# Layer 0 of a four-layer graph network: the one-hots of four edge tiles from one comparison, tiles innermost

## The chip, the cores and the metric

The kernel runs on one core of one Trainium2 chip. The metric is the device time of one execution in microseconds (us). Engines are called as in the profile: PE is TensorE's matrix unit, PEld its weight loads, DVE is VectorE, ACT is ScalarE, POOL is GpSimd, SP is SyncE.

## The reference

Four graph layers run one after the other over 6,250 nodes with 128 features and 206,250 edges sorted by destination; after each, the result is added to the features and normalised. The change lies in the first layer (layer 0), which averages the features of each node's sources:

```python
agg = segment_sum(x[src], dst, num_segments=n)
deg = segment_sum(ones(src.shape[0]), dst, num_segments=n)
mean_neigh = agg / maximum(deg, 1.0)[:, None]
out = x @ w_self.T + b_self + mean_neigh @ w_neigh.T + b_neigh
x = layernorm(x + out)
```

Layer 1 runs an MLP over each edge and sums it by destination, layer 2 sums node and edge features over neighbours, layer 3 is graph attention with four heads. They are the same before and after.

## The kernel before

The edges are cut into NT = 1612 tiles of 128 edges (one edge per partition), the nodes into NB = 49 blocks of 128. Since edges are sorted by destination, a tile touches only S = 7 destination slots. GT = 18 tiles make a group with 18 x 7 = 126 slots; there are NS = 90 groups.

Layer 0 doesn't gather. For each tile `q` it builds two one-hot matrices in bf16 and multiplies them. `hotU` (128 edges x 128) marks the source's row within its block (`src & 127`, called `low`). `hotV` (128 edges x 343) marks the pair of source block and slot (`(src >> 7) * 7 + slot`, less `CMID`, called `code`). Their product on TensorE, `dense_adjacency` (L662), is a 128 x 343 matrix of edge counts in PSUM. ScalarE copies it into the group's matrix `AT` in `dense_counts` (L642). When the 18 tiles of a group are there, `dense_sums` (L681) multiplies that matrix with the node features: 49 matmuls of 258 columns for a group, spread over the next 18 tiles, so that each tile has two or three of them behind its L662. GpSimd stores each group's matrix to DRAM (`atab`, L773) for layer 2; `AT` has two buffers, so ScalarE's first copy of group s waits for the store of group s-2.

Each engine runs one loop over the place `q`, in an order written out by hand. At place q VectorE makes the hots of tile q (L622 and L624), and at fixed distances the steps of the nodes' tail (division, residual, norm: L695 to L719), the group's small sums (L655) and its node one-hots (L558). The hots sit in a ring of NU = 8 tiles: VectorE waits for the adjacency matmul of tile q-8 (`d.adj`) before it writes tile q, TensorE for both hots of q (`d.hot`) and for the copy out of one of three PSUM banks (`d.count`). `codes` (L600 to L609) makes `low` and `code` as float32 for 18 tiles in five instructions, at the middle of the group before. At the even places 10 to 26 VectorE also makes the low halves of the features (L790, nine parts). Before all this, the prologue splits the features (L385, L391), casts the two ranges `ioc` and `iob` to bf16 (L375, L376) and prepares bias rows (L395, L397, L401).

The two instructions that make the one-hots of a tile compare a bf16 range with one scalar for each partition:

```python
e.tensor_scalar(hotU[:, q % NU, :], iob[:, :], low[:, s % 2, i:i + 1], None, ALU.is_equal)
e.tensor_scalar(hotV[:, q % NU, 0:S * NB], ioc[:, :], code[:, s % 2, i:i + 1], None, ALU.is_equal)
```

Of the kernel before, what the change touches and what calls it, by code (L numbers as in the profile page):

```python
# [9 lines left out]
I32 = mybir.dt.int32  # L10
FR = mybir.dt.float32r
BF = mybir.dt.bfloat16
ALU = mybir.AluOpType
ACT = mybir.ActivationFunctionType
AX = mybir.AxisListType
P = 128
G = 4
# [3 lines left out]
S = 7  # L21
GT = P // S
# [7 lines left out]
def plan(n_nodes, n_edges, n_rand):  # L30
    nb = -(-n_nodes // P)
    nt = -(-n_edges // (P * G)) * G
    lo, hi = [], []
    for b in range(nb):
        ends = []
        for d, sign in ((b * P, -1), (min((b + 1) * P, n_nodes), 1)):
            q = d / n_nodes
            mean = d + n_rand * q
            ends.append(mean + sign * (5 * (n_rand * q * (1 - q)) ** 0.5 + 2))
        lo.append(max(0, int(ends[0] // P)))  # L40
        hi.append(min(nt, int(-(-ends[1] // P))))
    lo[0], hi[-1] = 0, nt
    first = [min(b for b in range(nb) if lo[b] <= t < hi[b]) for t in range(nt)]
    last = [max(b for b in range(nb) if lo[b] <= t < hi[b]) for t in range(nt)]
    return nb, nt, lo, hi, first, last


def groups(nt, first, last):

    ns = -(-nt // GT)  # L50
    return ns, [first[GT * s] for s in range(ns)], [last[min(GT * s + GT, nt) - 1] for s in range(ns)]
# [53 lines left out]
def build(nc, n_nodes, n_edges, n_rand, a, out):  # L105
    NB, NT, LO, HI, FIRST, LAST = plan(n_nodes, n_edges, n_rand)
    NS, B0, B1 = groups(NT, FIRST, LAST)
# [5 lines left out]
    NEA = 5  # L113
    ND = 5
    NK = 4
    NU = 8
    CMID = S * NB // 2
    CB = 6
    NCB = -(-NB // CB)
# [7 lines left out]
    END = [min(GT * s + GT, NT) - 1 for s in range(NS)]  # L127
# [6 lines left out]
    with ctx:  # L134
        def sb(name, shape, dt=F32, c=ctx):
            return c.enter_context(nc.sbuf_tensor(name, shape, dt))

        def sem(name):
            return ctx.enter_context(nc.semaphore(name))
# [14 lines left out]
        slot = sb("slot", [P, NS * GT])  # L154
# [2 lines left out]
        hs = sb("hs", [P, NB, HB])  # L157
        nd = sb("nd", [P, NB, 4])
        am = sb("am", [P, 8])
        iob = sb("iob", [P, P], BF)  # L160
        ioc = sb("ioc", [P, S * NB], BF)
        iota = sb("iota", [P, 256])
        npcol = sb("npcol", [P, NB])
        oh2 = sb("oh2", [P, ND, 256], FR)
# [67 lines left out]
        s_mid = sem("s_mid")  # L232
# [19 lines left out]
        mid = sb("mid", [P, S * NB], c=pre)  # L252
        odd = sb("odd", [P, GT], c=pre)
        hflat = hs[:, :, :].rearrange("p a b -> p (a b)")
# [3 lines left out]
        def x_part(c):  # L258
            return slice(CB * c, min(CB * c + CB, NB))
# [73 lines left out]
        def prep_vector(e):  # L333
# [38 lines left out]
            e.tensor_scalar(node[0:SL, :], node[0:SL, :], small[0:SL, 0:1], None, ALU.add).then_inc(s_prep_v, 1)  # L372
            e.tensor_scalar(par[:, 1:2], par[:, 0:1], -1.0, 1.0, ALU.mult, ALU.add).then_inc(s_prep_v, 1)
            e.wait_ge(s_mid, 1)
            e.tensor_copy(ioc[:, :], mid[:, :]).then_inc(s_mid, 1)  # L375
            e.tensor_copy(iob[:, :], iota[:, 0:P]).then_inc(s_mid, 1)  # L376

            e.wait_ge(s_x, 16)
            for c in range(NCB + 1):
                if c < NCB:  # L380
                    b = x_part(c)
                    u = over0[:, c % 2, 0:(b.stop - b.start) * P].rearrange("p (b f) -> p b f", f=P)
                    if c >= 2:
                        e.wait_ge(s_xhi, 2 * c - 1)
                    e.scalar_tensor_tensor(out=u, in0=xs[:, b, :], scalar=SPLIT, in1=xs[:, b, :], op0=ALU.mult,  # L385
                                           op1=ALU.subtract).then_inc(s_xhi, 1)
                if c:
                    b = x_part(c - 1)
                    u = over0[:, (c - 1) % 2, 0:(b.stop - b.start) * P].rearrange("p (b f) -> p b f", f=P)
                    e.wait_ge(s_xhi, max(1, 2 * c - 2))  # L390
                    e.scalar_tensor_tensor(out=xhl[:, b, 0:128], in0=xs[:, b, :], scalar=SPLIT, in1=u, op0=ALU.mult,  # L391
                                           op1=ALU.subtract).then_inc(s_xhi, 1)
# [57 lines left out]
        with nc.Block() as block:  # L450
            block.gpsimd(prep_pool)
            block.sync(prep_sync)
            block.vector(prep_vector)
            block.tensor(prep_tensor)
            block.scalar(prep_scalar)
# [3 lines left out]
        def expected():  # L459
# [22 lines left out]
            held1 = sb("held1", [P, NK, 2, 384], FR, c=l1)  # L482
            over1 = sb("over1", [P, 2, 384], c=l1)
            l1.close()
            o = NU * (P + 352) // 2
            gint, low, code = (hflat[:, o + 2 * GT * i:o + 2 * GT * (i + 1)].rearrange("p (u c) -> p u c", u=2)
                               for i in range(3))
            gint = gint.bitcast(I32)
            l3 = ExitStack()
            hots = sb("hots", [P, GT, S], c=l3)  # L490
            pk = sb("pk", [P, GT, 4], c=l3)
# [26 lines left out]

            rv1 = view(NR1, 384)
            hbf = hflat.bitcast(BF)  # L520
            hotU = hbf[:, 0:NU * P].rearrange("p (n c) -> p n c", n=NU)
            hotV = hbf[:, NU * P:NU * (P + 352)].rearrange("p (n c) -> p n c", n=NU)
            ADJ = bank[1], bank[4], bank[5]
            AT = tuple(at0[:, i, :].rearrange("p (b c) -> p b c", c=SL) for i in range(2))
            rv3 = ring[:, :].rearrange("p (t f) -> p t f", f=HROW)
# [65 lines left out]

            def codes(e, d, s):

                n = END[s] - GT * s + 1
                c = slice(GT * s, GT * s + n)
                if s:
                    e.wait_ge(d.code, 5 * s)
                e.tensor_scalar(gint[:, 0, 0:n], src[:, c], P - 1, None, ALU.bitwise_and).then_inc(d.code, 1)  # L600
                e.tensor_scalar(gint[:, 1, 0:n], src[:, c], 7, None, ALU.arith_shift_right).then_inc(d.code, 1)
                if s >= 2:
                    e.wait_ge(d.hot, 2 * (END[s - 2] + 1))
                e.wait_ge(d.code, 5 * s + 2)
                e.tensor_copy(low[:, s % 2, 0:n], gint[:, 0, 0:n]).then_inc(d.code, 1)
                e.scalar_tensor_tensor(out=code[:, s % 2, 0:n], in0=gint[:, 1, 0:n], scalar=float(S), in1=slot[:, c],
                                       op0=ALU.mult, op1=ALU.add).then_inc(d.code, 1)
                e.wait_ge(d.code, 5 * s + 4)
                e.tensor_scalar(code[:, s % 2, 0:n], code[:, s % 2, 0:n], -float(CMID), None, ALU.add).then_inc(d.code, 1)  # L609

            def dense_hots(e, d, q):
                if q == 0:
                    codes(e, d, 0)
                elif q % GT == GT // 2 and q // GT + 1 < NS:
                    codes(e, d, q // GT + 1)
                if q < NT:
                    s, i = q // GT, q % GT
                    if i == 0:
                        e.wait_ge(d.code, 5 * s + 5)
                    if q >= NU:  # L620
                        e.wait_ge(d.adj, q - NU + 1)
                    e.tensor_scalar(hotU[:, q % NU, :], iob[:, :], low[:, s % 2, i:i + 1], None, ALU.is_equal).then_inc(  # L622
                        d.hot, 1)
                    e.tensor_scalar(hotV[:, q % NU, 0:S * NB], ioc[:, :], code[:, s % 2, i:i + 1], None,  # L624
                                    ALU.is_equal).then_inc(d.hot, 1)

            def dense_blank(e, d, q):
                n = END[NS - 1] - GT * (NS - 1) + 1
# [27 lines left out]

            def dense_adjacency(e, d, q):
                if q < NT:
                    e.wait_ge(d.hot, 2 * q + 2)
                    if q >= 3:  # L660
                        e.wait_ge(d.count, q - 2)
                    e.matmul(ADJ[q % 3][:, 0:S * NB], hotU[:, q % NU, :], hotV[:, q % NU, 0:S * NB], start=True,  # L662
                             stop=True).then_inc(d.adj, 1)

            LAG0 = 1
# [115 lines left out]
            def vector0(e):  # L781
                e.wait_ge(s_src, 16)
                e.wait_ge(s_mid, 3)
                e.wait_ge(s_prep_v, 31)
                e.memset(xhl[:, :, 256:YW].bitcast(F32), 1.0).then_inc(s_ones0, 1)
                for q in range(N0):
                    c = (q - LOW0) // 2
                    if (q - LOW0) % 2 == 0 and 0 <= c < NCB:
                        b = x_part(c)
                        e.tensor_tensor(xhl[:, b, 128:256], xs[:, b, :], xhl[:, b, 0:128].bitcast(F32), ALU.subtract).then_inc(  # L790
                            s_xlo, 1)
                    dense_hots(e, d0, q)
                    dense_blank(e, d0, q)
                    if q - 8 in KEEPS0:
                        halves_added(e, d0, KEEPS0[q - 8])
                    if q in NODES0:
                        node_hots(e, NODES0[q], d0.node, d0.add, ND, B1[max(0, NODES0[q] - ND)] + 1)
                    for b, k in W0.get(q, []):
                        vector_post0(e, b, k)
# [9 lines left out]
            def tensor0(e):  # L809
                e.wait_ge(s_ones0, 1)  # L810
                for q in range(N0):
                    dense_adjacency(e, d0, q)
                    dense_sums(e, d0, q)
                    for b in LASTS.get(ADDS0.get(q), []):
                        add_nodes(e, b, 129, 128, d0.node, d0.kept, 1, s_mean0, 6, d0.add)
                    for b, k in W0.get(q, []):
                        tensor_post0(e, b, k)
# [979 lines left out]
        with nc.If(strays == 0):  # L1797
            expected()
# [67 lines left out]
```

## Time and profile before

| | us |
|---|---|
| median of three runs | 6451.55 |
| lowest and highest | 6450.44, 6462.29 |
| span of the profiled execution, from its first to its last instruction | 5707.4 |
| median less the span (before the first and after the last instruction) | 744.15 |
| layer 0's adjacency matmuls, from the first to the last start | 50.0 to 948.1 |

The profiled execution has no time of its own on record beside its span, so the working is made against the span and carried over to the median: whatever the span gains or loses, the median does. Layer 0 takes some 900 us of the span; layer 1 follows to about 3,040, layer 2 to about 3,640, and layer 3 fills the rest. In a timeline the starts of two neighbouring instructions tell the engine's pace; the time of one is longer than the pace, since instructions overlap in the pipeline.

### The profile page before, as it was taken

What the parts mean: (1) busy time and instruction counts of PE and PEld (TensorE: products, weight loads), DVE (VectorE), ACT (ScalarE), POOL (GpSimd) and SP (SyncE); (2) the same over time, 40 slices, a digit from 0 to 9 for tenths busy, and PEclk for the clock granted to TensorE, in tenths of its full rate; (3) what the DMA queues carried; (4) which work ended last, traced back from release to release, by engine and by line L of the source; (5) the groups of instructions that cost most, each with busy time, mean ns of one, the idle gap of its engine ahead of it and who ended that gap; (6) DMA issues with size and microseconds to landing.
All of it is one profiled execution on the core that took longest, in us unless ns stands there. A gap on an engine that the chain in (4) does not pass through costs nothing.

```text
span 5707.4 us, 76723 instructions
## 1 busy us (share of the span) xinstructions
PE 4531.6 (79%) x25589; PEld 3717.3 (65%) x25589; DVE 2795.5 (49%) x10327; ACT 1993.7 (35%) x4098; POOL 3118.8 (55%) x3336
## 2 busy tenths in 40 slices
PE   6999998999999999999998999644545544544544
PEld 5999997667677777767768999634444444444444
DVE  8999996333333333433345444333443443443444
ACT  5888886222222222222224555211111121111112
POOL 0000002777777777777770000377777777777775
PEclk9999999999999999999999999777777777677777
DMA  6777777777767777777766777422222222222221
GB/s 153 170 167 165 165 168 178 210 212 210 210 210 211 209 212 208 212 208 212 209 189 191 243 244 246 123 55 56 56 56 56 56 56 56 56 56 56 57 56 43
DMA packets 479979, 843.08 MB, mean 148 GB/s; under 512 B 73951, under 2 KB 302474, under 8 KB 468074
## 3 DMA queue, kind: packets, MB, share of 16 engines
q0 software_dynamic: 141920, 462.69, 32.3%
q1 hardware_dynamic: 323562, 365.74, 21.0%
q10 hardware_dynamic: 14112, 9.74, 0.5%
q8 instruction: 214, 3.51, 0.2%
q14 instruction: 171, 1.40, 0.1%
HBM read 682.70 MB, written 155.18 MB: 147 GB/s over the span
## 4 chain that ended last, share of the span: by engine, by line
PE 49%; POOL 26%; issue 10%; DMA 7%; DVE 6%; ACT 1%; ACTq 0%; POOLq 0%; DVEq 0%
POOL ring L536 26%; PE bank L1196 9%; PE bank L1028 9%; PE bank L681 8%; PE bank L1015 7%; PE bank L662 4%; DMA ring<-ptab,src 4%; DMA ring<-htab,src 2%; PE bank L1478 2%; PE bank L1514 2%; PE bank L1507 1%; PE bank L576 1%; DVE ring L1405 1%; DMA atab<-at 1%; PE bank L1485 1%
## 5 line engine op out<-in xcount | busy, mean ns | idle before, releaser
L536 POOL DMA_INDIRECT ring<-htab,src x1612 | 1527.4, 947 | 503.1 <-issue 472.2
L536 POOL DMA_INDIRECT ring<-ptab,src x1612 | 1526.8, 947 | 498.6 <-issue 440.7
L1028 PE MATMUL bank<-ring,oh 128*126 128x384 f32 x3224 | 1213.7, 488 | 0.0
L982 DVE TENSOR_TENSOR ring<-bank,ring 128x512 f32<-128x512 f32 x806 | 529.9, 685 | 1231.8 <-DMA ring<-ptab,src 1227.7
L1015 PE MATMUL bank<-w1e,ea 128*128 128x256 f32 x3224 | 845.7, 385 | 46.2 <-DVE ring L982 37.3
L998 ACT ACTIVATE ring<-ring 128x1024 f32<-128x1024 f32 x403 | 425.6, 1056 | 1252.8 <-DVE ring L982 1252.8
L1015 PEld LDWEIGHTS bank<-w1e,ea 128*128 128x128 f32 x3224 | 601.1, 190 | 354.0 <-DVE ring L982 119.8
L681 PE MATMUL bank<-xhl,at 128*126 128x258 f32 x4410 | 815.3, 325 | 1.0 <-ACT at L642 1.0
L1514 PE MATMUL bank<-ring,oh 128*126 128x132 f32 x3224 | 589.8, 316 | 244.9 <-DVE ring L1405 244.3
L642 ACT ACTIVATE at<-bank 128x343 fp32r<-128x343 f32 x1612 | 731.2, 489 | 140.7 <-PE bank L662 61.6
L1028 PEld LDWEIGHTS bank<-ring,oh 128*126 128x126 f32 x3224 | 589.8, 188 | 199.8
L1514 PEld LDWEIGHTS bank<-ring,oh 128*126 128x126 f32 x3224 | 492.2, 215 | 333.1 <-DVE ring L1405 314.7
L681 PEld LDWEIGHTS bank<-xhl,at 128*126 128x126 f32 x4410 | 695.6, 192 | 3.5 <-ACT at L642 1.2
L1470 PE MATMUL bank<-ident,pk 128*72 128x128 f32 x90 | 38.4, 427 | 753.5 <-ACT pk L1428 753.5
L1196 PE MATMUL bank<-yhl,adj 128*126 128x256 f32 x4410 | 565.3, 286 | 11.8 <-DVE yhl L1085 11.8
L1196 PEld LDWEIGHTS bank<-yhl,adj 128*126 128x126 f32 x4410 | 538.4, 188 | 14.7 <-DVE yhl L1085 10.5
L773 POOL DMA_DIRECT2D atab<-at x90 | 51.0, 567 | 892.3 <-ACT at L642 892.3
L662 PE MATMUL bank<-hs 128*128 128x343 bf16 x1612 | 515.8, 321 | 16.0 <-DVE hs L624 8.6
L1470 PEld LDWEIGHTS bank<-ident,pk 128*72 128x72 f32 x90 | 12.2, 136 | 776.6 <-ACT pk L1428 776.6
L624 DVE TENSOR_SCALAR hs<-ioc,hs 128x343 bf16<-128x343 bf16 x1612 | 492.3, 305 | 0.0
L622 DVE TENSOR_SCALAR hs<-iob,hs 128x128 bf16<-128x128 bf16 x1612 | 401.1, 249 | 43.9 <-PE bank L662 30.3
L1054 POOL MEMSET oh<- 128x4788 f32 x1 | 4.1, 4088 | 643.9 <-PE bank L1196 643.9
(268 smaller groups left out, 5298.0 us busy)
## 6 DMA issues: line engine op xcount, KB each, us to landing
atab<-at POOLq DMA_DIRECT2D x90, 1543.5 KB, 9.6
ring<-ea_r SPq DMA_DIRECT2D x403, 256.0 KB, 4.0
ea<-ea_t SPq DMA_DIRECT2D x403, 256.0 KB, 3.1
adjb<-atab SPq DMA_DIRECT2D x180, 535.5 KB, 4.7
adjb<-atab SPq DMA_DIRECT2D x90, 472.5 KB, 4.2
ring<-ptab,src POOLq DMA_INDIRECT x1612, 3.5
ring<-htab,src POOLq DMA_INDIRECT x1612, 2.5
ptab<-pO ACTq DMA_DIRECT2D x49, 128.0 KB, 4.6
```

Of the source, the lines that this page charges most:

```text
L536: return e.indirect_dma_start(o, None, table, bass.IndirectOffsetOnAxis(ap=src[:, t:t + 1], axis=0))
L622: e.tensor_scalar(hotU[:, q % NU, :], iob[:, :], low[:, s % 2, i:i + 1], None, ALU.is_equal).then_inc(d.hot, 1)
L624: e.tensor_scalar(hotV[:, q % NU, 0:S * NB], ioc[:, :], code[:, s % 2, i:i + 1], None, ALU.is_equal).then_inc(d.hot, 1)
L642: e.activation(AT[s % 2][:, :, S * i:S * i + S], ADJ[t % 3][:, 0:S * NB].rearrange("p (b j) -> p b j", j=S), ACT.Copy).then_inc(d.count, 1)
L662: e.matmul(ADJ[q % 3][:, 0:S * NB], hotU[:, q % NU, :], hotV[:, q % NU, 0:S * NB], start=True, stop=True).then_inc(d.adj, 1)
L681: m = e.matmul(SUM[g % 2][0:SL, 0:YW], AT[g % 2][:, h, :], xhl[:, h, :], start=h == 0, stop=h == NB - 1)
L982: e.tensor_tensor(group1(gi, m % 2), MLP[m % 3][:, :].rearrange("p (g f) -> p g f", g=2), group1(gi, m % 2), ALU.add).then_inc(s_edge, 1)
L998: e.activation(group1(gi), group1(gi), ACT.Relu).then_inc(s_relu, 1)
L1015: w = e.matmul(MLP[m % 3][:, 256 * i:256 * i + 256], ea[:, gi % NEA, 2 * h + i, :], w1e[:, :], start=True, stop=True)
L1028: e.matmul(SUM[s % 2][0:SL, 0:384], slots_of(s, i), rv1[:, t // G % NR1, t % G, :], start=i == 0, stop=t == END[s]).then_inc(s_sum1, 1)
L1196: m = e.matmul(SUM[g % 2][0:SL, 0:256], adj[:, u % 3, c * SL:c * SL + SL], yhl[:, h, :], start=h == 0, stop=h == NB - 1)
L1514: e.matmul(SUM[g % 2][0:SL, 0:HROW], slots_of(g, k), rv3[:, t % (NRING * G), :], start=k == 0, stop=t == END[g]).then_inc(s_sum3, 1)
```

## The change

`iob` and `ioc` become 128 x (128 x 4) and 128 x (343 x 4), each value four times in a row. For every fourth tile, two `tensor_tensor` instructions, both operands bf16, compare them with the codes of four tiles at once, so the hots of four tiles lie interleaved, tiles innermost. The ring holds NQ = 3 of these fours, twelve tiles. `low` and `code` are bf16 rows for all 1612 tiles, made in five pieces (64 tiles, then four of 387) at the places 0, 8, 16, 24 and 32. TensorE reads both operands of L662 at a stride of four elements (8 bytes).

```diff
-    NU = 8
+    NQ = 3
+    SEGS = [0, 64] + [64 + -(-(NT - 64) * k // 4) for k in range(1, 5)]
-        iob = sb("iob", [P, P], BF)
-        ioc = sb("ioc", [P, S * NB], BF)
+        iob = sb("iob", [P, P, G], BF)
+        ioc = sb("ioc", [P, S * NB, G], BF)
-            e.tensor_copy(ioc[:, :], mid[:, :]).then_inc(s_mid, 1)
-            e.tensor_copy(iob[:, :], iota[:, 0:P]).then_inc(s_mid, 1)
+            e.tensor_copy(ioc[:, :, :], mid[:, :].unsqueeze(2).broadcast_to([P, S * NB, G])).then_inc(s_mid, 1)
+            e.tensor_copy(iob[:, :, :], iota[:, 0:P].unsqueeze(2).broadcast_to([P, P, G])).then_inc(s_mid, 1)
...
+            def codes(e, d, k):
+                c, n = slice(SEGS[k], SEGS[k + 1]), SEGS[k + 1] - SEGS[k]
+                if k:
+                    e.wait_ge(d.code, 5 * k)
                 e.tensor_scalar(gint[:, 0, 0:n], src[:, c], P - 1, None, ALU.bitwise_and).then_inc(d.code, 1)
                 e.tensor_scalar(gint[:, 1, 0:n], src[:, c], 7, None, ALU.arith_shift_right).then_inc(d.code, 1)
+                e.wait_ge(d.code, 5 * k + 2)
+                e.tensor_copy(low[:, c], gint[:, 0, 0:n]).then_inc(d.code, 1)
+                e.scalar_tensor_tensor(out=codef[:, 0:n], in0=gint[:, 1, 0:n], scalar=float(S), in1=slot[:, c], op0=ALU.mult,
+                                       op1=ALU.add).then_inc(d.code, 1)
+                e.wait_ge(d.code, 5 * k + 4)
+                e.tensor_scalar(code[:, c], codef[:, 0:n], -float(CMID), None, ALU.add).then_inc(d.code, 1)
 
             def dense_hots(e, d, q):
                 if q == 0:
                     codes(e, d, 0)
-                elif q % GT == GT // 2 and q // GT + 1 < NS:
-                    codes(e, d, q // GT + 1)
-                    if q >= NU:
-                        e.wait_ge(d.adj, q - NU + 1)
-                    e.tensor_scalar(hotU[:, q % NU, :], iob[:, :], low[:, s % 2, i:i + 1], None, ALU.is_equal).then_inc(
-                        d.hot, 1)
-                    e.tensor_scalar(hotV[:, q % NU, 0:S * NB], ioc[:, :], code[:, s % 2, i:i + 1], None,
-                                    ALU.is_equal).then_inc(d.hot, 1)
+                if q % 8 == 0 and 1 <= q // 8 < len(SEGS) - 1:
+                    codes(e, d, q // 8)
+                if q < NT and q % G == 0:
+                    k = q // G
+                    e.wait_ge(d.code, 5 * next(i for i in range(1, len(SEGS)) if q < SEGS[i]))
+                    if k >= NQ:
+                        e.wait_ge(d.adj, G * (k - NQ + 1))
+                    for o, i, c, n in ((hotU, iob, low, P), (hotV, ioc, code, S * NB)):
+                        e.tensor_tensor(o[:, k % NQ, :, :], i[:, :, :], c[:, q:q + G].unsqueeze(1).broadcast_to([P, n, G]),
+                                        ALU.is_equal).then_inc(d.hot, 1)
...
-                    e.wait_ge(d.hot, 2 * q + 2)
+                    e.wait_ge(d.hot, 2 * (q // G) + 2)
                     if q >= 3:
                         e.wait_ge(d.count, q - 2)
-                    e.matmul(ADJ[q % 3][:, 0:S * NB], hotU[:, q % NU, :], hotV[:, q % NU, 0:S * NB], start=True,
+                    e.matmul(ADJ[q % 3][:, 0:S * NB], hotU[:, q // G % NQ, :, q % G], hotV[:, q // G % NQ, :, q % G], start=True,
                              stop=True).then_inc(d.adj, 1)
```

## Rows read from the trace of the kernel before

**Rows 1.** The page: its first line, and one of the costliest groups.

```profile
span 5707.4 us, 76723 instructions
...
L982 DVE TENSOR_TENSOR ring<-bank,ring 128x512 f32<-128x512 f32 x806 | 529.9, 685 | 1231.8 <-DMA ring<-ptab,src 1227.7
```

**Rows 2.** Busy time by stretch of layer 0: PE, PEld, DVE, ACT, POOL, clock, DMA.

```profile
48.00:56.00 8.00, 4.62 (x12) 1.24 (x12) 7.20 (x37) 4.17 (x11) 0.00 (x0) 0.50 0.00 1
56.00:64.00 8.00, 4.51 (x14) 1.90 (x14) 8.00 (x26) 4.17 (x11) 0.74 (x1) 0.50 0.12 25
64.00:68.00 4.00, 4.00 (x20) 3.56 (x19) 3.90 (x17) 2.34 (x5) 0.00 (x0) 0.53 1.17 247
68.00:76.00 8.00, 8.00 (x63) 7.20 (x62) 7.83 (x45) 7.11 (x18) 0.71 (x1) 1.00 0.36 76
76.00:950.00 874.00, 866.01 (x6693) 786.73 (x6692) 807.50 (x4254) 743.47 (x1843) 49.55 (x88) 1.00 0.78 167
```

**Rows 3.** Groups of instructions by line, 76 to 950 us.

```profile
L681 PE MATMUL bank<-xhl,at 128*126 128x258 f32 x4289 | 794.0, 325 | 1.0 <-ACT at L642 1.0
L642 ACT ACTIVATE at<-bank 128x343 fp32r<-128x343 f32 x1572 | 713.8, 489 | 129.6 <-PE bank L662 51.2 <-DMA atab<-at 33.6 <-PE bank L681 18.3
L681 PEld LDWEIGHTS bank<-xhl,at 128*126 128x126 f32 x4288 | 676.4, 191 | 3.3 <-ACT at L642 1.2
L662 PE MATMUL bank<-hs 128*128 128x343 bf16 x1570 | 499.8, 318 | 7.0 <-DVE hs L622 3.9 <-ACT at L642 2.6 <-DVE hs L624 0.2
L624 DVE TENSOR_SCALAR hs<-ioc,hs 128x343 bf16<-128x343 bf16 x1567 | 478.6, 305 | 0.0
L622 DVE TENSOR_SCALAR hs<-iob,hs 128x128 bf16<-128x128 bf16 x1567 | 389.9, 249 | 43.8 <-PE bank L662 30.3
L662 PEld LDWEIGHTS bank<-hs 128*128 128x128 bf16 x1570 | 150.9, 96 | 82.7 <-DVE hs L622 5.4 <-DVE hs L624 3.0 <-issue 1.7
```

**Rows 4.** Timeline of PE in the steady part: start, us, instruction.

```profile
503.34 0.32 PE L662 MATMUL bank<-hs 128*128 128x343 bf16 x1
503.38 0.64 PE L681 MATMUL bank<-xhl,at 128*126 128x258 f32 x3
503.86 0.32 PE L662 MATMUL bank<-hs 128*128 128x343 bf16 x1
503.90 0.52 PE L681 MATMUL bank<-xhl,at 128*126 128x258 f32 x2
504.26 0.32 PE L662 MATMUL bank<-hs 128*128 128x343 bf16 x1
```

**Rows 5.** Timeline of PE, one of its longest waits.

```profile
623.83 0.31 PE L662 MATMUL bank<-hs 128*128 128x343 bf16 x1 [1.08 <-ACT at L642]
```

**Rows 6.** Timeline of ACT at the same place.

```profile
623.20 0.48 ACT L642 ACTIVATE at<-bank 128x343 fp32r<-128x343 f32 x1 [1.84 <-DMA atab<-at]
```

**Rows 7.** DMA issues: KB each, median us from issue to landing.

```profile
atab<-at POOLq DMA_DIRECT2D x90, 1543.5 KB, 9.6
```

**Rows 8.** Timeline of DVE in the first places of layer 0.

```profile
48.69 0.11 DVE L600 TENSOR_SCALAR hs<-src 128x18 int32<-128x18 int32 x1
...
49.41 0.25 DVE L622 TENSOR_SCALAR hs<-iob,hs 128x128 bf16<-128x128 bf16 x1
...
52.85 0.17 DVE L600 TENSOR_SCALAR hs<-src 128x18 int32<-128x18 int32 x1
...
53.50 0.25 DVE L622 TENSOR_SCALAR hs<-iob,hs 128x128 bf16<-128x128 bf16 x1
...
53.88 0.95 DVE L790 TENSOR_TENSOR xhl<-xs,xhl 128x768 fp32r<-128x768 f32 x1
54.75 0.25 DVE L622 TENSOR_SCALAR hs<-iob,hs 128x128 bf16<-128x128 bf16 x1
```

**Rows 9.** Timeline of PE: the adjacency matmul of tile 36.

```profile
73.26 0.32 PE L662 MATMUL bank<-hs 128*128 128x343 bf16 x1
```

**Rows 10.** Groups of DVE by line, 0 to 60 us: the wait behind the casts.

```profile
L397 DVE TENSOR_TENSOR hs<-hs,bup 128x896 f32<-128x896 f32 x1 | 1.1, 1093 | 3.3 <-ACT bup L435 3.3
```

More of the change, by code:

```diff
@@ L484, in expected @@
             l1.close()
[L485 to L488, printed above, removed]
+            WHOT = NQ * G * (P + S * NB) // 2
+            LSEG = max(b - a for a, b in zip(SEGS, SEGS[1:]))
+            gint = hflat[:, WHOT + NT:WHOT + NT + 2 * LSEG].rearrange("p (u c) -> p u c", u=2).bitcast(I32)
+            codef = hflat[:, WHOT + NT + 2 * LSEG:WHOT + NT + 3 * LSEG]
             l3 = ExitStack()
@@ L520, in expected @@
             hbf = hflat.bitcast(BF)
-            hotU = hbf[:, 0:NU * P].rearrange("p (n c) -> p n c", n=NU)
-            hotV = hbf[:, NU * P:NU * (P + 352)].rearrange("p (n c) -> p n c", n=NU)
+            hotU = hbf[:, 0:NQ * G * P].rearrange("p (n c g) -> p n c g", n=NQ, g=G)
+            hotV = hbf[:, NQ * G * P:NQ * G * (P + S * NB)].rearrange("p (n c g) -> p n c g", n=NQ, g=G)
+            low, code = (hbf[:, 2 * WHOT + i * NT:2 * WHOT + (i + 1) * NT] for i in range(2))
             ADJ = bank[1], bank[4], bank[5]
@@ L590, in places @@
                 return max(at) + 1, hots, nodes, keeps, adds, at
[L594 to L599, printed above, removed]
+            def codes(e, d, k):
+                c, n = slice(SEGS[k], SEGS[k + 1]), SEGS[k + 1] - SEGS[k]
+                if k:
+                    e.wait_ge(d.code, 5 * k)
                 e.tensor_scalar(gint[:, 0, 0:n], src[:, c], P - 1, None, ALU.bitwise_and).then_inc(d.code, 1)
                 e.tensor_scalar(gint[:, 1, 0:n], src[:, c], 7, None, ALU.arith_shift_right).then_inc(d.code, 1)
[L602 to L609, printed above, removed]
+                e.wait_ge(d.code, 5 * k + 2)
[4 more added lines that the diff above has]
+                e.tensor_scalar(code[:, c], codef[:, 0:n], -float(CMID), None, ALU.add).then_inc(d.code, 1)
             def dense_hots(e, d, q):
@@ L613, in dense_hots @@
                     codes(e, d, 0)
-                elif q % GT == GT // 2 and q // GT + 1 < NS:
-                    codes(e, d, q // GT + 1)
[L616 to L619, printed above, removed]
-                    if q >= NU:
-                        e.wait_ge(d.adj, q - NU + 1)
-                    e.tensor_scalar(hotU[:, q % NU, :], iob[:, :], low[:, s % 2, i:i + 1], None, ALU.is_equal).then_inc(
-                        d.hot, 1)
-                    e.tensor_scalar(hotV[:, q % NU, 0:S * NB], ioc[:, :], code[:, s % 2, i:i + 1], None,
-                                    ALU.is_equal).then_inc(d.hot, 1)
+                if q % 8 == 0 and 1 <= q // 8 < len(SEGS) - 1:
[8 more added lines that the diff above has]
+                                        ALU.is_equal).then_inc(d.hot, 1)
             def dense_blank(e, d, q):
```

## The prediction

> **What bounds the kernel now.** I read the page first: the span is 5707.4 us, the median of the runs 6451.55, so 744.15 us lie outside the span and are touched by nothing here [rows 1]. All edits lie in layer 0, between 48 and 950 us. The table by stretch comes next [rows 2]. The reader is to see two regimes. From 76 to 950 us PE is busy 866.01 of 874.00 us: its idle time there is 8.0 us in all, while DVE is busy 807.50, ACT 743.47. From 48 to 64 us it is the other way round: DVE is busy 15.2 of 16 us, PE 9.1, at a granted clock of 0.50 (1.2 GHz); the clock is back at 1.00 (2.4 GHz) only in the stretch from 68.
>
> Then, whether PE's busy time is its own pace: the PE timeline shows an L662 and three L681 starting over after 0.52 us (503.34 to 503.86), and an L662 with two L681 after 0.40 [rows 4]. So an L681 costs 0.12 us and an L662 0.40 - 0.24 = 0.16. At 2.4 GHz, 258 columns are 0.1075 us and 343 columns 0.143. That is a matmul pace with 0.02 us to spare, not one set by waits. A group of 18 tiles holds 49 L681, 13 threes and 5 twos: (13 x 0.52 + 5 x 0.40) / 18 = 0.487 us a tile.
>
> Last, what the 8.0 us wait for. The groups by line name DVE for part of it [rows 3], but at the longest wait PE stood 1.08 us for ScalarE's copy [rows 5], and that copy had stood 1.84 us for the store of `atab` [rows 6]; ScalarE waits 33.6 us for that store in all [rows 3]. The store lands 9.6 us after its issue [rows 7], and a group lasts 874 / 1570 x 18 = 10.0 us. So the next thing behind PE is the store and the copies, not the one-hots. DVE itself waits 30.3 us for PE: its ring of eight tiles is full [rows 3].
>
> **The change part by part.**
>
> *The hots, from 76 us on.* Before, a tile's pair costs DVE 0.38 us (53.50 to 53.88) [rows 8]. The trace has no 16-bit `tensor_tensor`. Its float32 ones give a slope: 512 elements take 685 ns [rows 1], 768 take 0.95 us [rows 8], so (0.95 - 0.685) / 256 = 1.04 ns an element, and the next instruction starts 0.87 us after a 768 (53.88 to 54.75) [rows 8]: 768 x 1.04 = 0.80, so 0.07 fixed. Upper bound, one element a tick: 512 x 1.04 + 0.07 = 0.60 and 1372 x 1.04 + 0.07 = 1.50, together 2.10 for four tiles, 0.525 a tile. Lower, two a tick: 0.34 + 0.785 = 1.12, 0.28 a tile. The 16-bit L622 and L624 differ by 56 ns for 215 elements [rows 3], 0.26 ns each, four a tick; the engine does pack 16-bit data, so I take two a tick, since a second operand also has to be read. The Trainium skill ("VectorE: DVE Perf Modes", "The perf-mode tier table") gives the bf16 `tensor_tensor` the double rate and no more; no row shows it. DVE then saves 0.10 us a tile, 157 us over 1570 tiles, and the codes' 88 small pieces of 0.65 us (52.85 to 53.50) [rows 8], 57 us. That is worth **nothing**, because PE hides all of DVE's work there. PE's waits there give at most the 8.0 us of idle time back, and I take 0 of them, since their cause is the store.
>
> *Four tiles at a time, ring of twelve.* DVE begins four k when PE has done four k-3, so PE has eight tiles, 8 x 0.487 = 3.9 us, before it needs four k, against 1.12 us of hots. Behind DVE's new wait stand the tail's steps, and their due times are 1 to 10 places from PE's; DVE is now 8 to 12 places ahead, before it was at most 8. Cost 0. If the cover went (hots at 0.525 us), see rival C.
>
> *The start.* Here DVE sets the pace, and the four long code pieces are now all due in it. A small piece costs 0.65 us; 369 more elements cost, at 1.04 ns in all five instructions, 1.92 us more (upper), or at 0.26 ns in the four with one source and 1.04 in the fifth, 0.77 (lower). I take 1.8 us a piece, between 1.42 and 2.57. The first piece, 64 elements, takes the 0.72 us of before (48.69 to 49.41) [rows 8] and 0.14. Sum until the hots of tiles 32 to 35 are there: start 48.69, first piece 0.86, four pieces 7.2, nine fours of hots 9 x 1.12 = 10.1, eight L790 of 0.87 and a short one 7.2: 74.05. PE then does four tiles in 4 x 0.487 = 1.95, and tile 36 starts at 76.0, against 73.26 [rows 9]: **+2.7 us**, between +1.2 and +5.8 by the pieces' bounds. From there PE is the pace again. The hots of tiles 16 to 27 come in bursts, so PE may get its 2.4 GHz later than at 68 us; for each L681 it misses that costs about 0.1 us, and I add **1 us**, between 0 and 4 (some forty of them).
>
> *The casts.* They grow from 471 to 1884 elements in the prologue: at most 1413 x 1.04 = 1.5 us more. Behind them DVE waits 3.3 us for ScalarE's `bup` [rows 10], which covers it: 0. Without that cover it would be 1.5.
>
> *TensorE's strided reads.* No row of this trace has a strided operand on PE. Moving operand: nothing (lower), or each of the 343 columns costs two, 0.143 us a tile, 1612 x 0.143 = 230 us (upper). The nearest row is L681, 4-byte elements side by side at one column a tick: two of our 2-byte elements at 8 bytes' distance span the same 16 bytes as four of those. I take 0, being nearer to a pace that the rows show for half the density. The Trainium skill ("SBUF — State Buffer", "Door 1: The DMA port swizzle") says that SBUF is read in lines of 16 bytes and that two hits in a line suffice for the full rate; eight bytes give just two, and the sum by it is the same 0. Weight load: L662's takes 96 ns, L681's 191 [rows 3]. If the stride makes the first like the second, 0.095 x 1612 = 153 us in full view (upper); but the 191 ns loads lie behind matmuls that follow each other at 0.12 us [rows 4], and L662's load has a 258-column matmul ahead of it, so 0.
>
> Sum: 5707.4 + 2.7 + 1 = 5711.1 for the span, **6455 us** for the median. The own range of this case: 6451.5 + 1.2 - 8.0 = 6445 to 6451.5 + 5.8 + 4 = 6461.
>
> **The rivals.**
>
> *A, TensorE pays a little* (0.08). A load a tenth in view, or a column in ten delayed: 10 to 28 ns a tile, 16 to 45 us, 6472 to 6500. For it: PE has only 0.02 us to spare at L662. It decides from 6 ns a tile on (9 us, with the start over 0.2%).
>
> *B, each column pays* (0.08). The moving read halves: 6455 + 230 = 6685, or half of that, 6570. For it: no row shows a strided read. Against it: the density argument above. The Trainium skill ("Vector Engine (DVE) Microarchitecture Reference", "Measured stream behaviour on trn2") has a rule for VectorE's ports by which only pairs of neighbouring 4-byte words keep the full rate; carried over to TensorE it would be this rival.
>
> *C, the comparison isn't packed* (0.06). The innermost run is only four elements and the codes are a repeated row. Then DVE needs 807.5 + 1570 x 0.145 - 57 = 978 us where PE needs 866: DVE sets the pace, +104 us, and nine fours at 0.98 more, +9 at the start: 6568. It decides where a tile's hots cost more than 0.38 + (874 - 807.5 + 57) / 1570 = 0.46 us.
>
> *D, the other side: faster* (0.07). PE's 0.52 and 0.40 us stand above their columns (0.465 and 0.358) by 0.054 and 0.042 us, up to 80 us in all [rows 4]. If part of that is TensorE held up in SBUF by DVE, which now issues a half instruction a tile for two, it comes back: a third would be 26 us, 6430. Against it: no row shows one engine's reads slowing another's, and the excess may as well be the switch from one matmul to the next. It decides from 0.011 us a tile.
>
> **How the numbers follow.** Main case 0.71, A 0.08, B 0.08, C 0.06, D 0.07. A measurement of this kernel tells 0.2%, 13 us, from no change. The main case gives no change 0.63, slower 0.06, faster 0.02; A, B, C slower 0.22; D faster 0.05 and no change 0.02. Faster 0.07, same 0.65, slower 0.28. The range 6444 to 6500 holds the main case, A and a part of D, about 0.81; B and C lie outside.
>
> **What would show it.** In the changed profile: the hots' `tensor_tensor` near 0.34 and 0.8 us in pace (C: 0.6 and 1.5); DVE's busy time from 76 us down by some 200 us, PE's unchanged near 99%; L662 and three L681 still at 0.52 us (A, B: more; D: less); tile 36 near 76 us; ScalarE's waits for the store of `atab` still there. I am wrong if the pace of 0.52 moves, or if the start costs more than 10 us.

## The result: 6697 us, 3.8% slower

The changed kernel took 6696.68 us (median of four, 6688.77 to 6704.66) against 6451.64 before: a ratio of 1.038, 95% interval 1.0365 to 1.0395. The prediction was no change, 6455 us; the time lies where rival B put it, at 6685 us.

One word on spans first. The chips differ in how fast layers 1 and 3 get their gathered rows: on some the median of the kernel before lies at 6452 to 6469 us, on two others at 5721 and 5723. Its profile [rows 1] has the gathers of the fast kind, where its span is its time but for 5 us; a second profile of it shows that below. So the 744 us that I put outside the span do not exist as such. Layer 0 lasts the same on both kinds: two kernels below whose layers 0 are alike from tile 36 on (`stride2` and `late_codes`) take 882.1 us for it on one kind and 881.9 on the other. Every ratio below is taken on one chip.

The page of the changed kernel begins:

```profile
span 6692.9 us, 74103 instructions
```

Busy time after, first the start and then the rest of layer 0 (PE, PEld, DVE, ACT, POOL, clock, DMA share, GB/s), the answer to [rows 2]:

```profile
68.00:76.00 8.00, 7.12 (x34) 5.93 (x34) 6.96 (x17) 4.19 (x9) 0.00 (x0) 0.65 0.48 101
...
76.00:1190.00 1114.00, 1113.47 (x6711) 910.69 (x6710) 608.05 (x1474) 795.95 (x1849) 46.82 (x88) 1.00 0.61 131
```

The steady part grew from 874 to 1114 us for the same matmuls, at the same granted clock of 1.00. PE is idle for 0.5 us of it, where it was for 8.0. DVE fell from 807.50 to 608.05 us, as forecast. The change did what it does to DVE, and PE, the bound, became slower at the same work. Which part of the work, the groups by line show, beside [rows 3]:

```profile
L679 PE MATMUL bank<-xhl,at 128*126 128x258 f32 x4298 | 1042.0, 377 | 0.5 <-ACT at L640 0.5
...
L640 ACT ACTIVATE at<-bank 128x343 fp32r<-128x343 f32 x1579 | 757.8, 487 | 318.0 <-PE bank L660 246.3 <-PE bank L679 52.2 <-issue 0.3
L660 PE MATMUL bank<-hs 128*128 128x343 bf16 x1579 | 749.0, 474 | 0.0
L622 DVE TENSOR_TENSOR hs<-ioc,hs 128x1372 bf16<-128x1372 bf16 x393 | 340.8, 867 | 0.0
L660 PEld LDWEIGHTS bank<-hs 128*128 128x128 bf16 x1579 | 180.2, 114 | 72.2
L622 DVE TENSOR_TENSOR hs<-iob,hs 128x512 bf16<-128x512 bf16 x393 | 166.8, 424 | 407.8 <-PE bank L660 407.2
```

The adjacency matmul (L660 now, L662 before) went from 318 to 474 ns, its weight load from 96 to 114. ScalarE no longer waits for the store of `atab`: a group now lasts 1114 / 1579 x 18 = 12.7 us, and the store lands 9.4 us after its issue. PE's timeline, against [rows 4]:

```profile
599.97 0.47 PE L660 MATMUL bank<-hs 128*128 128x343 bf16 x1
600.02 0.78 PE L679 MATMUL bank<-xhl,at 128*126 128x258 f32 x3
600.64 0.47 PE L660 MATMUL bank<-hs 128*128 128x343 bf16 x1
600.70 0.66 PE L679 MATMUL bank<-xhl,at 128*126 128x258 f32 x2
601.20 0.48 PE L660 MATMUL bank<-hs 128*128 128x343 bf16 x1
```

L660 and three sums start over after 0.67 us instead of 0.52, with two sums after 0.56 instead of 0.40. L679 is recorded longer (377 ns instead of 325), but its own pace is unchanged: a tile with three sums still takes 0.12 us more than one with two. Below, "pace" is the median of these gaps for tiles with three sums, over the whole layer: 0.519 us before, 0.676 after. The difference, 0.157 us, times 1576 tiles is 247 us; the stalls that went give some 10 back: from tile 36 to the last tile's matmul it takes 1111.75 us against 874.8, 237 more. The start adds 5.0 (tile 36 at 78.25 us, against [rows 9]). Together 242, of the 245 measured.

### The profile page after: what moved, and what is told of

It reads as the page before. It is cut to its first block, busy times and chain, and to the rows that moved or that the text cites. A ratio compares the mean times of both kernels' runs of the same rounds, so it can differ in the third digit from the quotient of the medians.

```text
span 6692.9 us, 74103 instructions
## 1 busy us (share of the span) xinstructions
PE 5056.7 (76%) x25589; PEld 4043.5 (60%) x25589; DVE 2615.9 (39%) x7484; ACT 2045.8 (31%) x4098; POOL 3111.3 (46%) x3336
## 4 chain that ended last, share of the span: by engine, by line
PE 55%; another core or an unknown queue 23%; issue 10%; DVE 9%; ACT 2%; POOL 0%; DMA 0%; ACTq 0%; DVEq 0%
PE bank L1026 12%; PE bank L1013 10%; PE bank L679 8%; PE bank L1194 8%; PE bank L660 7%; PE bank L1512 2%; DVE ring L1403 2%; DVE ring L980 2%; PE bank L578 1%; PE bank L963 1%; PE bank L1476 1%; DVE tops L1258 1%; DVE top L1262 1%; PE bank L1505 0%
## 5 line engine op out<-in xcount | busy, mean ns | idle before, releaser
L679 PE MATMUL bank<-xhl,at 128*126 128x258 f32 x4410 | 1063.3, 376 | 0.5 <-ACT at L640 0.5
L679 PEld LDWEIGHTS bank<-xhl,at 128*126 128x126 f32 x4410 | 818.1, 205 | 130.6 <-ACT at L640 1.1
L1512 PE MATMUL bank<-ring,oh 128*126 128x132 f32 x3224 | 702.3, 364 | 248.1 <-DVE ring L1403 133.8
L1512 PEld LDWEIGHTS bank<-ring,oh 128*126 128x126 f32 x3224 | 602.7, 259 | 340.7 <-DVE ring L1403 176.7
L1026 PEld LDWEIGHTS bank<-ring,oh 128*126 128x126 f32 x3224 | 614.8, 196 | 266.0 <-issue 75.4
L660 PE MATMUL bank<-hs 128*128 128x343 bf16 x1612 | 763.2, 475 | 12.1 <-DVE hs L622 11.9
L1491 PE MATMUL bank<-hs,o2T 128*126 128x4 f32 x346 | 78.0, 329 | 507.3 <-ACT o2T L1441 360.8
L1476 PE MATMUL bank<-rT,sel 72*126 72x128 f32 x720 | 172.8, 416 | 339.6 <-issue 241.9
L1491 PEld LDWEIGHTS bank<-hs,o2T 128*126 128x126 f32 x346 | 73.0, 295 | 525.7 <-ACT o2T L1441 374.0
L1476 PEld LDWEIGHTS bank<-rT,sel 72*126 72x126 f32 x720 | 148.3, 307 | 359.5 <-issue 255.6
L1258 DVE TENSOR_TENSOR tops<-bank,away 126x512 f32<-126x512 f32 x90 | 62.3, 692 | 773.4 <-remote 726.3
```

The costliest lines, as they stand in the source:

```text
L660: e.matmul(ADJ[q % 3][:, 0:S * NB], hotU[:, q // G % NQ, :, q % G], hotV[:, q // G % NQ, :, q % G], start=True, stop=True).then_inc(d.adj, 1)
L679: m = e.matmul(SUM[g % 2][0:SL, 0:YW], AT[g % 2][:, h, :], xhl[:, h, :], start=h == 0, stop=h == NB - 1)
L1026: e.matmul(SUM[s % 2][0:SL, 0:384], slots_of(s, i), rv1[:, t // G % NR1, t % G, :], start=i == 0, stop=t == END[s]).then_inc(s_sum1, 1)
L1476: m = e.matmul(bank[5][0:SL, h * P:(h + 1) * P], sel[0:4 * n, h, :], rT[0:4 * n, :], start=True, stop=True)
L1491: m = e.matmul(bank[7][0:SL, 0:4], o2T[:, b - B0[f], :], hs[:, b, 132:136], start=b == B0[f], stop=b == B1[f])
L1512: e.matmul(SUM[g % 2][0:SL, 0:HROW], slots_of(g, k), rv3[:, t % (NRING * G), :], start=k == 0, stop=t == END[g]).then_inc(s_sum3, 1)
```

## Experiments

**Which operand, or VectorE after all.** Three kernels keep every instruction of the change and alter only where TensorE reads in the four's region. Flat means that an operand's elements are read side by side, and so are a mix of four tiles' one-hots; such a kernel leaves the right counts out.

```diff
+            flatU = hbf[:, 0:NQ * G * P].rearrange("p (n g c) -> p n g c", n=NQ, g=G)
+            flatV = hbf[:, NQ * G * P:NQ * G * (P + S * NB)].rearrange("p (n g c) -> p n g c", n=NQ, g=G)
...
-e.matmul(ADJ[q % 3][:, 0:S * NB], hotU[:, q // G % NQ, :, q % G], hotV[:, q // G % NQ, :, q % G], ...)
+e.matmul(ADJ[q % 3][:, 0:S * NB], flatU[:, q // G % NQ, q % G, :], hotV[:, q // G % NQ, :, q % G], ...)   # weights_flat
+e.matmul(ADJ[q % 3][:, 0:S * NB], hotU[:, q // G % NQ, :, q % G], flatV[:, q // G % NQ, q % G, :], ...)   # moving_flat
+e.matmul(ADJ[q % 3][:, 0:S * NB], flatU[:, q // G % NQ, q % G, :], flatV[:, q // G % NQ, q % G, :], ...)  # both_flat
```

> As the changed kernel, but TensorE reads the stationary operand of L662 (now L662 of this file) as 128 elements side by side from the same four's region, and the moving one still at a stride of four. The one-hots of wrong elements meet, so the counts are not the reference's; every instruction is the same in number and size. Theory M (the moving read pays for each column): a tile with three sums stays near the 0.675 us of the changed kernel, 6685 to 6697 us. Theory W (the strided weight load is what holds TensorE): back to 0.52 us a tile, 6455 us. Both in halves: about 6575 us.

Measured: 6691.86 us against 6469.27, ratio 1.0342 (1.0323 to 1.036), pace 0.665. With no strided weight load nearly the whole cost is still there: theory M. In its timeline a tile with three sums starts over after 0.66 us:

```profile
600.11 0.46 PE L662 MATMUL bank<-hs 128*128 128x343 bf16 x1
...
600.77 0.46 PE L662 MATMUL bank<-hs 128*128 128x343 bf16 x1
```

> The mirror of the run before: the moving operand is read side by side, the stationary one at a stride of four; the counts are not the reference's. Theory M: 0.52 us a tile with three sums, L662 back at 0.32 us, 6450 to 6465 us. Theory W: near 0.675 us and 6697 us. If the weight load's 114 ns instead of 96 come into view, 18 ns a tile, 29 us more: 6485 us.

Measured: 6489.7 us, ratio 1.003 (1.0019 to 1.004), pace 0.538. The matmul is back at 0.34 us and less, and the load's 18 ns come into view in full: 0.019 x 1612 = 31 us, of which the time shows 20, since PE's waits for ScalarE shrink from 6.0 to 1.5 us and ScalarE's for the store from 28.9 to 20.9. This is rival A, in the size it had (10 to 28 ns a tile), but beside the moving operand it is small; with both strided only 0.011 us of it shows (0.676 less 0.665); why not all of it stays open.

> Both operands read side by side; the counts are not the reference's. What is left of the change is VectorE's: hots by fours, the ring of twelve, five code pieces at the start, longer casts. Prediction's own sum: 6455 us, tile 36 near 76 us, between 6445 and 6461. Rival (waiting by fours costs TensorE something, apart from how it reads): above 6465 us.

Measured: 6468.82 us, ratio 0.9999 (0.9989 to 1.0009), pace 0.519. That it lies above the rival's 6465 us is the chip's doing: before takes 6469.27 there. From tile 36 to the last tile it needs 873.5 us, before 874.8, so waiting by fours costs TensorE nothing. Its groups from 76 to 950 us:

```profile
L642 ACT ACTIVATE at<-bank 128x343 fp32r<-128x343 f32 x1577 | 715.5, 489 | 129.2 <-PE bank L662 54.7 <-DMA atab<-at 28.9 <-PE bank L681 18.2
...
L662 PE MATMUL bank<-hs 128*128 128x343 bf16 x1576 | 502.4, 319 | 6.4 <-ACT at L642 6.0
L624 DVE TENSOR_TENSOR hs<-ioc,hs 128x1372 bf16<-128x1372 bf16 x393 | 340.6, 867 | 0.0
L624 DVE TENSOR_TENSOR hs<-iob,hs 128x512 bf16<-128x512 bf16 x392 | 165.6, 423 | 206.8 <-PE bank L662 203.8
```

With VectorE's part alone the layer is what the prediction said of it: 208 us of VectorE's busy time (807.50 to 599.58 in 874) buy nothing, ScalarE waits for the store as before, and nearly all of PE's waits at L662 are for ScalarE.

**How far apart may columns lie.** First a kernel that computes the right result with two tiles interleaved.

```diff
-    NQ = 3
+    NQ = 6
+    H = 2        # in place of G for iob, ioc, hotU, hotV, dense_hots and dense_adjacency
```

> The one-hots of two tiles interleaved instead of four, six pairs in the ring, so TensorE reads both operands at a stride of two elements, 4 bytes; the computation is whole. Theory M1 (TensorE reads 4-byte words side by side, and pays where the next column is not in the same or the next word): full pace, 0.52 us, 6455 us. Theory M2 (any element stride halves the rate): 0.675 us and 6690 us. Theory M3 (the cost grows with the bytes between columns): between, near 0.6 us and 6570 us. VectorE: a pair of hots 0.20 + 0.43 us for two tiles.

Measured: 6473.86 us, ratio 1.001 (1.000 to 1.002), pace 0.526. Columns 4 bytes apart are nearly free (0.007 us a tile), so a stride as such costs next to nothing, and M2 and M3 fall.

Four more leave the stationary operand flat and give the moving one other patterns. They were run once each, and so were the two behind them; the pace, a median over some thousand tiles, is what counts. All six leave the right counts out too.

```diff
+            def moving(k):
+                o = NQ * G * P + k % NQ * G * S * NB
+                return hbf[:, o:o + 1029].rearrange("p (c g) -> p c g", g=3)[:, :, 0]                                          # bytes6
+                return hbf[:, o:o + 1376].rearrange("p (c g) -> p c g", g=8)[:, :, 0].unsqueeze(1).broadcast_to([P, 2, 172])   # bytes16
+                return hbf[:, o:o + 1376].rearrange("p (c g) -> p c g", g=8)[:, :, 0:2]                                        # runs2
+                return hbf[:, o:o + 1376].rearrange("p (c g) -> p c g", g=16)[:, :, 0:4]                                       # runs4
```

> The changed kernel with the stationary operand read side by side and the moving one of 343 elements at a stride of three, 6 bytes, from the first part of the four's region; the counts are not the reference's. Measured so far for a tile with three sums: 0.519 us at 2 bytes, 0.526 at 4 (both operands), 0.665 at 8. Theory G (TensorE fetches aligned pieces of 8 bytes, one in two ticks at 2.4 GHz, so a column costs two ticks where it is alone in its piece): four columns lie in three pieces, 1.5 ticks each, 0.519 + 0.071 = 0.59 us, about 6580 us. Theory H (from a stride of three elements on, every column costs two ticks): 0.665 us, 6695 us. Theory L (only lines of 16 bytes count, two hits are enough; 8 bytes would then have to be dear for another reason): 0.52 us.

> The same with a stride of eight elements, 16 bytes: 172 columns, read twice for 344; the counts are not the reference's. Theory G and theory H: 0.665 us again and about 6695 us, a column alone in its piece of 8 bytes costs no more when the next piece is farther off. Theory L2 (the cost grows with the lines of 16 bytes that are fetched, twice as many as at 8 bytes): 0.95 us a tile and about 7150 us.

> The moving operand in 172 runs of two elements, 16 bytes from run to run, 344 columns; the counts are not the reference's. Theory G: two columns in each piece of 8 bytes, full pace, 0.52 us, 6470 us. Theory H2 (each hop of 8 bytes or more costs a tick): 0.519 + 172 / 2400 = 0.59 us, 6585 us. Theory of the word (only a column's own 4 bytes count and must lie next to the last): 0.59 us too.

> The moving operand in 86 runs of four elements, 8 bytes, 32 bytes from run to run, 344 columns; the counts are not the reference's. Theory G: full pace, 0.52 us, 6470 us. Theory H2: 0.519 + 86 / 2400 = 0.555 us, 6530 us.

Measured: 6572.81, 7168.46, 6692.53 and 6469.6 us (before on that chip 6463.16), pace 0.598, 0.967, 0.665 and 0.528. In the run at 16 bytes the timeline reads:

```profile
599.92 0.76 PE L665 MATMUL bank<-hs 128*128 128x344 bf16 x1
599.96 1.08 PE L684 MATMUL bank<-xhl,at 128*126 128x258 f32 x3
600.89 0.77 PE L665 MATMUL bank<-hs 128*128 128x344 bf16 x1
```

Theory G, with which I had gone in, got 6 bytes and the run of four right and fails twice: 16 bytes cost far more than 8, and two columns in one piece of 8 bytes aren't at full pace where the next pair is 16 bytes on. Theory H says 0.665 for the first two, not 0.598 and 0.967, and the theories of hops (H2) give 0.59 and 0.555 for the last two, not 0.665 and 0.528. Only L2, which counted lines at 16 bytes, was near there (0.95). What fits all is a count of 16-byte lines. That gave a new theory, L4, one line in four ticks of 2.4 GHz, and two runs that could break it.

```diff
+                return hbf[:, o + 6:o + 1382].rearrange("p (c g) -> p c g", g=16)[:, :, 0:4]                                   # runs4_split
+                return hbf[:, o:o + 1376].rearrange("p (c g) -> p c g", g=16)[:, :, 0].unsqueeze(1).broadcast_to([P, 4, 86])   # bytes32
```

> As the run with 86 runs of four elements 32 bytes apart, but read from 12 bytes further on; the counts are not the reference's. The fours' regions lie 2744 bytes apart, which is 8 more than a multiple of 16, so in the fours with k mod 3 of 0 and 2 each run of 8 bytes now crosses from one line of 16 bytes into the next, while with k mod 3 of 1 it lies within one (if the array itself begins on a line). Theory L4 (TensorE gets one line of 16 bytes in four ticks of 2.4 GHz, 1.67 ns, and a column costs no less than one tick): 0.665 us a tile where the runs cross, 0.528 where they don't. Rival (only the distance between runs counts): 0.528 everywhere, 6470 us.

> 86 columns at a stride of 32 bytes, read four times for 344; the counts are not the reference's. Theory L4: one line for each column as at 16 bytes, 0.967 us a tile, 7168 us. Rival (the cost goes on growing with the bytes between columns): near 1.5 us a tile and over 8000 us.

Measured: 5866.41 us against 5720.75 on that chip, and 6445.9. The first gives 0.664 us for the fours with k mod 3 of 0 and 2, and 0.527 for those with 1, as L4 said for an array that begins on a line. In its timeline the change from one kind of four to the other is seen in the middle of a row of like instructions:

```profile
600.63 0.47 PE L665 MATMUL bank<-hs 128*128 128x344 bf16 x1
...
601.18 0.33 PE L665 MATMUL bank<-hs 128*128 128x344 bf16 x1
...
602.77 0.33 PE L665 MATMUL bank<-hs 128*128 128x344 bf16 x1
...
604.07 0.47 PE L665 MATMUL bank<-hs 128*128 128x344 bf16 x1
```

Four in a row take 0.33 us (601.18 to 602.77), those before and behind 0.47, with the same pattern, moved by 8 bytes against the line. At 32 bytes the pace is 0.979 us, hardly above 16 bytes, so the lines aren't longer than 16 bytes either. Its 7168 us were forecast for the other kind of chip; over before it is 725 us, where the run at 16 bytes is 705. All paces together, with what L4 adds to 0.519 us (ticks a column above one, over 2.4):

| moving operand | columns in a line | L4 adds, us | measured |
|---|---|---|---|
| side by side | 8 | 0 | 0.519 |
| 4 bytes (both operands) | 4 | 0 | 0.526 |
| runs of 4, within a line | 4 | 0 | 0.528 |
| 6 bytes | 2.67 | 343 x 0.5 / 2400 = 0.071 | 0.598 |
| 8 bytes | 2 | 343 / 2400 = 0.143 | 0.665 |
| runs of 2, 16 bytes apart | 2 | 0.143 | 0.665 |
| runs of 4, across two lines | 2 | 0.143 | 0.664 |
| 16 bytes | 1 | 344 x 3 / 2400 = 0.430 | 0.967 |
| 32 bytes | 1 | 0.430 | 0.979 |

The sums come out within 9 ns in the rows down to two columns a line. At one column a line the measured pace is 18 and 30 ns above 0.949, so a line costs 1.72 and 1.75 ns there rather than 1.67; what the rest is stays open.

**The start, and the span of before.** The last pair tests the other term of the sum, and the 744 us. `late_codes` is the two-tile kernel with its long code pieces moved to where VectorE has time.

```diff
-    SEGS = [0, 64] + [64 + -(-(NT - 64) * k // 4) for k in range(1, 5)]
+    SEGS = [0, 64, 80, 96, 112, 128, 192, 320, 580, 840, 1100, 1360, NT]
```

> The kernel before once more, for its profile: its profiled span of 5707.4 us stood 744 us below its median, while the spans of the changed kernel and of the runs so far lie within 5 us of their times. Theory S (the profiled execution of before ran without something that all timed ones have): span near 6455 us, layer 0 as before (first to last adjacency matmul 898 us), and layers 1 and 3 longer, by waits of all engines for gathered rows. Theory O (the kernel before has 744 us outside its span): span 5707 us again.

> Two tiles interleaved (stride of 4 bytes, no cost for TensorE's columns), and the codes in pieces of 64, then 16 for each of the places 8 to 32, and the long ones at the places 40 to 96, where VectorE has time. Theory (the start costs what the long pieces take from VectorE): tile 36 starts four times some 1.1 us earlier than with two tiles and long pieces (77.5), near 73 us, and the time is 4 us below that run's, so 1.000 of before, 0.9995 to 1.0005. Rival (the start is set by the clock, which rises once the sums run): tile 36 stays near 77 us.

Measured: the kernel before took 5714.5 us on that chip, and its page begins

```profile
span 5709.6 us, 76723 instructions
```

so neither theory was quite right: the span is the first profile's again, and so is the time. It is the chip that differs, not the execution. In the profiles from the other chips the gathers of layers 1 and 3 stand 1.25 us apart as on this one, but mostly every twelfth, sixteenth or twentieth only after some 3.9 us. The changed kernel's profile has 211 such gaps, 621 us above 1.25 us each; the two profiles of before, `late_codes`, `runs4_split` and `bytes32` have none. Why those chips do so stays open. `late_codes` took 5731.14 us, ratio 1.0013 (1.0004 to 1.0022). Tile 36 starts at

```profile
72.67 0.33 PE L661 MATMUL bank<-hs 128*128 128x343 bf16 x1
```

where the two-tile kernel has it at 77.49 us and before at 73.26. By the profile the theory of the start holds, with 4.8 us won. The times don't show it: the two kernels ran on different chips, and their ratios of 1.001 and 1.0013 can't be told apart. The expected 1.000 isn't reached, since from tile 36 on the pace of 0.526 costs some 7 us (881.9 against 874.8). It is no version that beats before, and none of these runs points to one: PE is the bound, and the change has nothing for PE.

## Why the prediction was wrong

**The step that failed** is TensorE's strided moving read: "I take 0, being nearer to a pace that the rows show for half the density". It costs 0.146 us a tile (0.665 less 0.519, with the weights flat), the upper bound of 0.143 in full. The row was the right one and was read the wrong way round. L681 takes 258 columns of 4 bytes in 0.12 us [rows 4], which is four columns, one line of 16 bytes, in four ticks. L662 at a stride of 8 bytes would have needed a line in every two. Neither row shows lines coming that fast: side by side, bf16 needs one in eight ticks. "Span the same 16 bytes" compared bytes, where lines per column had to be compared, and the rows bounded the rate of lines from one side alone. With nothing to show a faster one, the upper end was the value to take. The chances followed: B had 0.08, and the range ended at 6500. B named the right size for this pattern, but its rule, every strided column pays, isn't what the runs show.

The Trainium skill ("SBUF — State Buffer", "Door 1: The DMA port swizzle") was right that the line has 16 bytes: the run across two lines shows it. By it two hits in a line are enough. Here they do not give the full rate at 2.4 GHz, four do; at 1.2 GHz two do. In the first places of layer 0, while the granted clock is 0.50, the changed kernel's tiles with three sums start

```profile
65.56 0.51 PE L660 MATMUL bank<-hs 128*128 128x343 bf16 x1
...
66.52 0.51 PE L660 MATMUL bank<-hs 128*128 128x343 bf16 x1
```

0.96 us apart, and those of the kernel that reads both operands flat

```profile
66.12 0.51 PE L662 MATMUL bank<-hs 128*128 128x343 bf16 x1
...
67.08 0.51 PE L662 MATMUL bank<-hs 128*128 128x343 bf16 x1
```

0.96 too. That bounds a line at two ticks of 1.2 GHz. The value itself is seen in the run at 16 bytes, at the same granted clock of 0.50, for two tiles with three sums:

```profile
70.13 0.81 PE L665 MATMUL bank<-hs 128*128 128x344 bf16 x1
...
71.38 0.81 PE L665 MATMUL bank<-hs 128*128 128x344 bf16 x1
```

1.25 us apart, 0.29 more for 344 columns, which is one more tick of 1.2 GHz (0.83 ns) for each. A line in four ticks of 2.4 GHz is one in two ticks of 1.2, 1.67 ns either way. The Trainium skill's rule for VectorE's ports ("Vector Engine (DVE) Microarchitecture Reference", "Measured stream behaviour on trn2"), which I named beside rival B, gave the right size for 8 bytes, but it isn't TensorE's. It lets runs of neighbouring words hop for free only where they start on an 8-byte boundary; in `runs4_split` all runs start 4 bytes past one, and those within a line cost nothing.

**Weight load.** "So 0" was nearly right: the load went from 96 to 114 ns, in view 0.019 us a tile alone and 0.011 beside the strided moving read.

**VectorE.** The hots at two a tick are borne out: 424 and 867 ns, starts 0.34 us apart within a four, as the sum had it, and rival C is out. "Worth nothing" is borne out by the run with both reads flat, at 0.9999. So is the low chance of rival D: there VectorE has half an instruction for a tile where it had two, and TensorE's pace is 0.519 us as before.

**The start.** The sum gave 76.0 us for tile 36, measured is 76.05 with flat reads. It isn't luck: the pieces of the sum are there too, with tile 32 at 74.10 us (sum 74.05) and 1.80 us for a long piece, here in the changed kernel:

```profile
51.21 0.35 DVE L601 TENSOR_SCALAR hs<-src 128x387 int32<-128x387 int32 x1
...
53.01 0.42 DVE L622 TENSOR_TENSOR hs<-iob,hs 128x512 bf16<-128x512 bf16 x1
53.34 0.87 DVE L622 TENSOR_TENSOR hs<-ioc,hs 128x1372 bf16<-128x1372 bf16 x1
```

The 1 us more for a late clock isn't seen there: the granted clock rises at 69.0 us instead of 67.8, but PE still has to wait for the hots of tile 32. In the changed kernel itself tile 36 starts at 78.25. From the same place on, twelve tiles take 8.95 us (69.30 to 78.25) where they take 6.19 with flat reads (69.86 to 76.05): the clock rises only at 73.7 us, so five of them still run at 1.2 GHz, and the seven after the rise already run at the slower pace. The casts stayed hidden: the wait for `bup` behind them shrank from 3.3 to 1.4 us, and layer 0 begins at 50.3 us instead of 50.0.

**The stalls on the store** were read rightly as ScalarE's and the store's. They vanish when PE slows down and stay when VectorE speeds up.

## What to carry to other kernels

Before an operand of TensorE is laid out with a stride, count its columns in each 16-byte line, from the line's own beginning: four or more are nearly free at 2.4 GHz, with fewer each line costs four ticks. Where TensorE is the bound, two bf16 tiles may be interleaved, four may not, and float32 may have no stride at all by the same count (not run here). When a change relieves one engine at the cost of how another reads, ask which of the two is the bound; here 200 us of VectorE were bought, at no use, for 240 of TensorE. And where a row bounds a rate from one side only, take the price at the unproven end, or give that end a larger chance.

## What the runs showed of the hardware

- TensorE's moving read gets one 16-byte line of SBUF in 1.67 ns, at 1.2 and at 2.4 GHz, nearly wherever the next line lies: 16 or 32 bytes on the paces are 0.967 and 0.979 us, 1.72 and 1.75 ns a line.
- Patterns with exactly four columns a line still cost 7 to 9 ns in 343 or 344 columns. What these are stays open.
- A 128-column bf16 weight load at a stride of 8 bytes takes 114 ns instead of 96, and the 18 ns come into view although a 258-column matmul runs ahead of it. At a stride of 4 bytes it takes 97.
- A bf16 comparison of two tensors on VectorE runs at two elements in 1.04 ns with one operand repeated in rows of four (512 and 1372 elements: starts 0.34 and 0.79 us apart), and also in rows of two (256 and 686 elements: 0.20 and 0.43 us).
